# Transformer layer of a graph network: both biases of the node product added by one product over 33 rows in place of two over one row

## The chip, the cores and the metric

The kernel runs on one core of one Trainium2 chip. The metric is the device time of one execution in microseconds (us). A measurement of this kernel is the median of several executions.

## The reference

A graph with 6250 nodes of 256 features and 106250 edges, sorted by destination. Two graph convolutions and a projection come first, then a graph attention layer, and last a transformer convolution. Only that last one bears on the change:

```python
q = x1 @ Wq + bq
k = x1 @ Wk + bk
v = x1 @ Wv + bv
logits2 = jnp.einsum('ec,ec->e', q[d2], k[s2]) * scale
alpha2 = _segment_softmax(logits2, d2, n)
out = jax.ops.segment_sum(v[s2] * alpha2[:, None], d2, num_segments=n)
out = out + x1 @ Wskip + bskip
return _prelu(out, prelu2_a)
```

## The kernel before

The kernel has a preparation (`prepare`) and four layer stages, each with its own instruction blocks for the five engines and a barrier over all engines behind it: two convolutions, the attention layer, and `transformer_layer`, which is changed. The preparation loads weights and biases with a list of transfers on SP's queue, and GpSimd clears and fills the constant tiles.

In `transformer_layer` the 106250 edges, padded, are 52 groups of 16 tiles of 128 edges. GpSimd gathers the source rows of each tile with an indirect transfer (832 of them, line 1520), 16 per group, into four buffers. A body handles three groups at different ages: the scores of group k, the softmax of group k - 1 and the aggregation of group k - 2. The tensor engine walks 16 slots in a body; in each it makes a score product (line 1851, 128x257) for a tile of group k and an aggregation product (line 1862, 128x257) for a tile of group k - 2. Other steps are hung in between at slots written out by hand:

```python
if agg and s == 4:
    node_turn(n2)
...
if agg and s == 8:
    node_multiply(n2)
if chain and s == 12:
    carry_factor()
```

The bodies 0 to 2 are written out, then a loop of 12 trips has four bodies each, and the remaining ones are written out again.

Aggregation follows linearity: the weighted sum of x1 rows of a node is divided by the sum of the weights and then multiplied with Wv, so that v is never stored per edge. `an` is the normalised sum of 128 nodes with its column of weight sums (256 + 1 columns), `own` the nodes' own rows. `node_turn` transposes both (line 1826) and the last column of `an` (line 1827) into a row. Scalar copies the first into `lt` (line 1964) and the row into `sa` (line 1965). `node_multiply` then adds six products into one PSUM tile: four over 128 rows (line 1833: `lt` with Wv and with Wskip, two halves each), one over one row, `sa` with bv (line 1834), and one over one row, ones with bskip (line 1835). Each f32 product shows in the trace as two weight loads and two matmul records. Vector (`node_halves`, lines 1624 and 1625) reads the result, applies the two halves of the PReLU and adds the residual; SP stores it. Vector also makes the dot products of the scores (line 1601), one per slot, each behind its score product, and the one-hot tiles (line 1589). Scalar weighs the one-hot tiles (line 1974), evicts their transposes (line 1958) and the finished sums (line 1970); the next body's first aggregation product waits for that eviction.

There are 53 node steps: one per group and one behind the last.

Of the kernel before, what the change touches and what calls it, by code (L numbers as in the profile page):

```python
# [20 lines left out]
ACT = mybir.ActivationFunctionType  # L21
P = 128
N = 6250
E = 106250
D = 256
# [10 lines left out]
RW = D + 1  # L36
# [3 lines left out]
NGW = NC // UW  # L40
NBW = 4
QW = 4
LN_EPS = 1e-5
BIG = 1.0e30
IOA = bass.IndirectOffsetOnAxis
# [67 lines left out]
def prepare(nc, m, a):  # L113
# [9 lines left out]
    with ExitStack() as c:  # L123
# [45 lines left out]
        @block.gpsimd  # L169
        def _(pool):  # L170
            y = Tally(pool, s_hd)
            nc.gpsimd.iota(m.iota[:], [[1, P]], base=0, channel_multiplier=0, allow_small_or_imprecise_dtypes=True)
            nc.gpsimd.iota(m.iotap[:], [[1, 1]], base=0, channel_multiplier=1, allow_small_or_imprecise_dtypes=True)
            nc.gpsimd.memset(m.ones[:], 1.0)
            nc.gpsimd.memset(m.ident[:], 0.0).then_inc(s_set, 1)
            pool.wait_ge(s_set, 1)
            nc.gpsimd.affine_select(out=m.ident[:], in_=m.ident[:], compare_op=ALU.not_equal, fill=1.0,
                                    base=0, pattern=[[-1, P]], channel_multiplier=1)
            nc.gpsimd.memset(m.eps[:], LN_EPS)
            nc.gpsimd.memset(zrow[:], 0.0).then_inc(s_set, 1)  # L180
            nc.gpsimd.memset(acc[:], 0.0).then_inc(s_set, 1)

            pool.wait_ge(s_acc, 1)
            hold(m, pool)
            for k in range(2):
                pool.wait_ge(s_half[k], 16)
                for g in range(k * HG, k * HG + HG):
                    d0, = load_wide(nc, m, pool, g, ("d0",))
                    to = acc[0:1, bass.ds(d0, P)]
                    y.chain(nc.gpsimd.tensor_tensor(to, to, part[0:1, (g % HG) * P:(g % HG) * P + P], ALU.add))  # L190

        @block.sync
        def _(sp):
            sp.dma_start(dstR[:], a["dst_cols"]).then_inc(s_ld, 16)
            with nc.allow_non_contiguous_dma(reason="first destination of each group"):
                sp.dma_start(d0w[0:1, 0:NGW], a["ends"][0:1, :, 0]).then_inc(s_ld, 16)
            sp.dma_start(m.wF[:, 0:NC], a["w_cols"]).then_inc(s_ld, 16)
            sp.dma_start(nxtI[:], a["next_cols"]).then_inc(s_ew, 16)
            sp.dma_start(endI[:], a["ends"].rearrange("k g p -> g k p")).then_inc(s_ew, 16)
            for k, n in enumerate(m.ROWS):  # L200
                sp.dma_start(m.rows[:, k, :], a[n].partition_broadcast(P)).then_inc(s_w, 16)
            sp.dma_start(m.srcI[:], a["src_cols"]).then_inc(s_w, 16)
            for t_, n in WLOADS:
                sp.dma_start(t_[:], a[n].rearrange("(k p) n -> p k n", p=P)).then_inc(s_w, 16)
            with nc.allow_non_contiguous_dma(reason="a column of biases"):
                sp.dma_start(bqc[:], a["bq"].rearrange("(k p) -> p k", p=P)).then_inc(s_w, 16)
            for t_, n in ((m.bv, "bv"), (m.bsk, "bskip")):
                sp.dma_start(t_[:], a[n].rearrange("(a n) -> a n", a=1)).then_inc(s_w, 16)

            sp.wait_ge(s_sums, 2)  # L210
            with nc.allow_non_contiguous_dma(reason="the blocks of a group's own rows and columns"):
                for gi in range(TB):
                    sp.dma_start(m.wsum.rearrange("(t g a b) -> g a t b", g=TB, a=A, b=B)[gi],
                                 sums[gi * A:gi * A + A, :, gi, :]).then_inc(s_wst, 16)
            sp.wait_ge(s_wst, 16 * TB)
            sp.dma_start(part[:], m.wsum[0:HG * P].rearrange("(a n) -> a n", a=1)).then_inc(s_half[0], 16)
            sp.wait_ge(s_set, 2)
            for t_, n in ((m.t3, AGW), (m.xa, D), (m.t2, D), (m.x1, RW), (m.t4, RW), (m.qk, RW)):
                sp.dma_start(t_[NP - P:NW, :].rearrange("(k p) n -> p k n", p=P), zrow[:, :, 0:n]).then_inc(s_st, 16)
            for t_, n in ((m.t1, D), (m.h0, RW)):  # L220
                sp.dma_start(t_[NP:NW, :], zrow[:, 0, 0:n]).then_inc(s_st, 16)
            sp.wait_ge(s_hd, HG)
            sp.dma_start(part[:], m.wsum[HG * P:NGW * P].rearrange("(a n) -> a n", a=1)).then_inc(s_half[1], 16)
            sp.wait_ge(s_hd, NGW)
            sp.dma_start(m.degd.rearrange("(a n) -> a n", a=1), acc[0:1, 0:NP]).then_inc(s_ast, 16)
            sp.wait_ge(s_ast, 16)
            sp.dma_start(degT[:], m.degd.rearrange("(t n) -> t n", n=P)).then_inc(s_dg, 16)
            for j in range(NLB):
                if j in ON_ACT:
                    sp.wait_ge(s_sca, ON_ACT.index(j) + 1)  # L230
                else:
                    sp.wait_ge(s_scd, j - (j + 1) // 2 + 1)
                sp.dma_start(rows(m.t1)[:, batch(j), :], h[:, batch(j), :]).then_inc(s_st, 16)
            sp.wait_ge(s_seg, 1)
            sp.dma_start(m.rmask.rearrange("(g e) -> g e", e=3 * (P + 1)), mks[:].rearrange("g k e -> g (k e)")).then_inc(s_st, 16)
            sp.wait_ge(s_st, 16 * (8 + NLB + 1))
# [539 lines left out]
def softmax_layer(nc, m, tag, gat):  # L776
# [11 lines left out]
    with ExitStack() as c:  # L788
# [396 lines left out]
        def _(pe):  # L1185
# [27 lines left out]
            def node_multiply(n):  # L1213
                pe.wait_ge(s_lt, n + 1)
                hold(m, pe)
                if gat:
                    for j in range(2):
                        nc.tensor.matmul(psO[:, 0:RW], lt[:, j, :], m.wqk[:, j, :], start=(j == 0), stop=False)
                    last = nc.tensor.matmul(psO[:, 0:RW], m.ones[0:1, :], m.bqk[:], start=False, stop=True)
                else:  # L1220
                    for j in range(4):
                        nc.tensor.matmul(psO[:, 0:D], lt[:, j, :], (m.wv, m.wsk)[j // 2][:, j % 2, :], start=(j == 0), stop=False)
                    nc.tensor.matmul(psO[:, 0:D], sa[:], m.bv[:], start=False, stop=False)
                    last = nc.tensor.matmul(psO[:, 0:D], m.ones[0:1, :], m.bsk[:], start=False, stop=True)
                last.then_inc(s_prod, 1)

            def rows_of(bp, u):
# [228 lines left out]
def transformer_layer(nc, m):  # L1456
# [4 lines left out]
    with ExitStack() as c:  # L1461
# [9 lines left out]
        F, W, W2, M, Lp = (sb(n, [P, UW]) for n in ("F", "W", "W2", "M", "Lp"))  # L1471
        T, z = sb("T", [P, 2, UW]), sb("z", [P, UW + 1])
        run, In, Lb, Out = sb("run", [1, P + 1]), sb("In", [1, P]), sb("Lb", [1, P + 1]), sb("Out", [1, P])
        own, xa, an, lt, sa = sb("own", [P, D]), sb("xa", [P, D]), sb("an", [P, RW]), sb("lt", [P, 4, P]), sb("sa", [1, P])
        v, o, rs = sb("v", [P, D]), sb("o", [P, D]), sb("rs", [P, 1])
        psA, psT, ps, psN, psO, psR = (psb("psA", [P, 2, 512]), psb("psT", [P, 2, 512]), psb("ps", [P, 512]),
                                       psb("psN", [P, 512]), psb("psO", [P, 512]), psb("psR", [P, 512]))
# [30 lines left out]
        @block.gpsimd  # L1508
        def _(pool):
            nc.gpsimd.memset(run[:], -BIG)  # L1510
            nc.gpsimd.memset(Lb[:], -BIG)
            nc.gpsimd.memset(stage[:], 0.0).then_inc(s_zero, 1)
            for g in range(NGW):
                b = g % NBW
                if g >= NBW:
                    pool.wait_ge(s_ok, g - NBW + 1)
                for u in range(UW):
                    if g >= NBW and u % QW == 0:
                        pool.wait_ge(s_aq, (g - NBW) * NQ + u // QW + 1)
                    pool.indirect_dma_start(G[:, b, u, :], None, m.t4, IOA(ap=m.srcI[:, g * UW + u:g * UW + u + 1],  # L1520
                                                                           axis=0)).then_inc(s_g[b][u // QW], 16)
# [64 lines left out]
        def _(dve):  # L1586
# [203 lines left out]
                if agg:  # L1790
                    aggregate_more(k - 2, nwin2, xb2, xb + nwin - 1 + xb2)

            dve.wait_ge(s_zero, 1)
            dve.sem_inc(s_agx, 1)
            nc.vector.tensor_copy(relx[:, 0], m.relW[:, 0:UW]).then_inc(s_relx, 1)
            nc.vector.tensor_copy(relx[:, 1], m.relW[:, UW:2 * UW]).then_inc(s_relx, 1)
# [10 lines left out]
        def _(pe):  # L1807
# [21 lines left out]
            def node_multiply(n):  # L1829
                pe.wait_ge(s_lt, n + 1)  # L1830
                hold(m, pe)
                for j in range(4):
                    nc.tensor.matmul(psO[:, 0:D], lt[:, j, :], (m.wv, m.wsk)[j // 2][:, j % 2, :], start=(j == 0), stop=False)  # L1833
                nc.tensor.matmul(psO[:, 0:D], sa[:], m.bv[:], start=False, stop=False)  # L1834
                nc.tensor.matmul(psO[:, 0:D], m.ones[0:1, :], m.bsk[:], start=False, stop=True).then_inc(s_prod, 1)  # L1835

            def body(k, kq, kh, b):
                logits, chain, agg, lead = parts(k)
# [114 lines left out]
        def _(act):  # L1953
# [7 lines left out]
            def node(n):  # L1961
                act.wait_ge(s_turn, n + 1)
                hold(m, act)
                nc.scalar.activation(lt[:].rearrange("p j e -> p (j e)"), psN[:], ACT.Copy)
                nc.scalar.activation(sa[:], psO[0:1, 256:256 + P], ACT.Copy).then_inc(s_lt, 1)

            def finish(n):
                act.wait_ge(s_x1, n + 1)
# [57 lines left out]
                            hold(m, act)  # L2026
                            finish(n2 + i)

            act.wait_ge(s_zero, 1)
            act.sem_inc(s_ev, 1)  # L2030
            for q in range(NQ - 1):
                evict(ohT, q, 0, s_T, s_oT)
# [5 lines left out]
def build(nc, a, out):  # L2038
    with ExitStack() as c:
        sb = lambda n, s, d=F32: c.enter_context(nc.sbuf_tensor(n, s, d))  # L2040
        m = Shared()
# [5 lines left out]
        m.steps, m.rcolW = sb("steps", [P, NT]), sb("rcolW", [P, NGW + 1])  # L2047
        m.ctw = sb("ctw", [1, NGW * TW + TW], I32)
        m.wv, m.wsk = (sb(n, [P, 2, D]) for n in ("wv", "wsk"))
        m.bv, m.bsk = sb("bvr", [1, D]), sb("bskr", [1, D])  # L2050
        m.rows = sb("rows", [P, len(m.ROWS), D])
        m.row = lambda n: m.rows[:, m.ROWS.index(n), :]
        dram = lambda n, s: nc.dram_tensor(n, s, F32, kind="Internal").ap()
# [58 lines left out]
```

## Time and profile before

| what | value |
|---|---|
| median of 3 runs | 5070.54 us (5068.86 to 5072.62) |
| profiled execution, its own time | 5070.05 us |
| span of the profiled execution | 5068.3 us |
| mean granted TensorE clock over the span | 0.817 |
| tensor engine busy over the span | 75% |
| vector, scalar, GpSimd busy | 52%, 17%, 64% |

The span is the time from the first to the last instruction of the profiled execution; the execution's own time lies 1.75 us above it. Names in the rows: PE is the tensor engine's matmul, PEld its weight load, DVE vector, ACT scalar, POOL GpSimd, SP the queue of transfers. L1834 is line 1834 of the kernel. The granted clock is a share of 2.4 GHz. A busy tensor engine is not one at its peak.

### The profile page before, as it was taken

How to read it: one execution, taken by the hardware profiler on the slowest of the kernel's cores; microseconds unless marked ns; L12 is line 12 of the kernel's file. 1: busy time of each engine (PE TensorE's matmuls, PEld its weight loads, DVE VectorE, ACT ScalarE, POOL GpSimd, SP SyncE). 2: the span in 40 equal slices, each digit the busy share in tenths (PEclk: the TensorE clock that was granted, in tenths of full speed). 3: DMA queues.
4: the chain of work that ended last, by engine and by line, in shares of the span. 5: the costliest groups of instructions: out<-in, count | busy, mean ns of one | idle time of the engine just before them, and what ended most of it. 6: DMA issues, size and time to landing. Idle time of an engine off the chain costs nothing. (4 is left out here: it accounts for less than half of the span.)

```text
span 5068.3 us, 77690 instructions
## 1 busy us (share of the span) xinstructions
PE 3792.3 (75%) x16038; PEld 2830.3 (56%) x16039; DVE 2616.1 (52%) x9965; ACT 873.7 (17%) x2343; POOL 3225.0 (64%) x3401
## 2 busy tenths in 40 slices
PE   2466666666767767767688888887869888888898
PEld 2244444443444544444566666666746666666666
DVE  8544444443333333333566666666745555555554
ACT  4100000000111111111111111111113333333333
POOL 3577777776777776662776666666437665566662
PEclk7778777777777777777788888878879999999999
DMA  5544444444444444442444444444224443344332
GB/s 158 139 129 131 130 131 129 129 133 115 135 133 132 135 132 123 124 126 63 115 125 113 107 109 104 105 106 108 79 67 129 118 112 105 104 110 109 107 107 57
DMA packets 323559, 585.83 MB, mean 116 GB/s; under 512 B 82891, under 2 KB 216070, under 8 KB 322950
## 3 DMA queue, kind: packets, MB, share of 16 engines
q0 software_dynamic: 159744, 440.25, 32.3%
q1 hardware_dynamic: 144153, 125.73, 8.1%
q10 hardware_dynamic: 19056, 12.87, 0.9%
q8 instruction: 245, 4.01, 0.4%
q14 instruction: 361, 2.96, 0.2%
HBM read 514.81 MB, written 63.78 MB: 114 GB/s over the span
## 5 line engine op out<-in xcount | busy, mean ns | idle before, releaser
L558 POOL DMA_INDIRECT g_G<-t,srcI x1664 | 1589.9, 955 | 550.2 <-issue 500.5
L729 PE MATMUL g_ps<-g_G,g_oh 128*128 128x256 f32 x3328 | 981.9, 453 | 262.9 <-DMA g_G<-t,srcI 239.4
L1520 POOL DMA_INDIRECT g_G<-t,srcI x832 | 792.1, 952 | 452.0 <-PE g_ps L1862 232.3
L859 POOL DMA_INDIRECT g_G<-t,srcI x832 | 801.5, 963 | 416.6 <-issue 242.1
L729 PEld LDWEIGHTS g_ps<-g_G,g_oh 128*128 128x128 f32 x3328 | 751.6, 231 | 501.6 <-issue 260.5
L612 DVE TENSOR_SCALAR g_oh<-iota,g_relx,g_wx 128x128 f32<-128x128 f32 x1664 | 461.0, 361 | 333.4 <-PE g_ps L729 319.9
L1851 PE MATMUL g_psA<-g_win,g_ohT 128*128 128x257 f32 x1664 | 539.2, 408 | 108.9 <-issue 74.3
L1601 DVE CUSTOM_DVE_ANT_0 g_junk<-g_G,g_psA 128x257 f32<-128x257 f32 x832 | 350.9, 422 | 507.9 <-PE g_psA L1851 392.3
L1862 PE MATMUL g_ps<-g_G,g_oh 128*128 128x257 f32 x1664 | 515.0, 393 | 44.3 <-ACT g_stage L1970 44.3
L1258 PE MATMUL g_ps<-g_Gp,g_oh 128*128 128x264 f32 x1664 | 519.1, 473 | 0.0
L1258 PEld LDWEIGHTS g_ps<-g_Gp,g_oh 128*128 128x128 f32 x1664 | 385.1, 240 | 84.8
L1862 PEld LDWEIGHTS g_ps<-g_G,g_oh 128*128 128x128 f32 x1664 | 317.5, 195 | 127.0 <-ACT g_oh L1974 58.5
L1851 PEld LDWEIGHTS g_psA<-g_win,g_ohT 128*128 128x128 f32 x1664 | 285.2, 197 | 176.8 <-issue 107.0
L1239 PE MATMUL g_psA<-g_win,g_ohT 128*128 128x4 f32 x1664 | 290.3, 310 | 2.6 <-issue 2.4
L1239 PEld LDWEIGHTS g_psA<-g_win,g_ohT 128*128 128x128 f32 x1664 | 285.2, 270 | 4.5 <-issue 3.4
L619 DVE TENSOR_TENSOR g_a<-g_stage,g_own 128x256 f32<-128x256 f32 x106 | 45.3, 427 | 451.1 <-ACT g_stage L770 451.1
L1974 ACT ACTIVATE g_oh<-g_oh,g_p 128x128 f32<-128x128 f32 x832 | 253.4, 388 | 6.5
L1958 ACT ACTIVATE g_ohT<-g_psT 128x512 f32<-128x512 f32 x208 | 124.2, 597 | 751.4 <-PE g_psT L1811 751.4
L1589 DVE TENSOR_SCALAR g_oh<-iota,g_relx 128x128 f32<-128x128 f32 x832 | 246.3, 298 | 0.0
L1163 DVE TENSOR_TENSOR g_Gp<-g_G,g_psP 128x1024 f32<-128x1024 f32 x208 | 238.8, 1201 | 0.0
L770 ACT ACTIVATE g_stage<-g_ps 128x256 f32<-128x256 f32 x104 | 39.8, 383 | 1145.2 <-PE g_ps L729 1145.2
L952 DVE TENSOR_SCALAR g_oh<-iota,g_relx 128x128 f32<-128x128 f32 x832 | 180.6, 302 | 73.7 <-DVE g_run L1134 36.4
(289 smaller groups left out, 4250.0 us busy)
## 6 DMA issues: line engine op xcount, KB each, us to landing
g_G<-t,srcI POOLq DMA_INDIRECT x3328, 2.8
g_own<-t SPq DMA_DIRECT2D x159, 128.0 KB
t<-g_t SPq DMA_DIRECT2D x53, 132.0 KB
g_rec<-t SPq DMA_DIRECT2D x53, 132.0 KB
g_rec<-h SPq DMA_DIRECT2D x53, 128.5 KB
x<-g_o SPq DMA_DIRECT2D x53, 128.5 KB
g_rec<-x SPq DMA_DIRECT2D x53, 128.5 KB
t<-g_t4r SPq DMA_DIRECT2D x53, 128.5 KB
```

What stands on the lines that cost most here:

```text
L558: pool.indirect_dma_start(G[:, b, u, :], None, table, IOA(ap=m.srcI[:, g * UW + u:g * UW + u + 1], axis=0)).then_inc(s_g[b][u // QW], 16)
L612: nc.vector.tensor_scalar(oh[:, u, :], m.iota[:], relx[:, u:u + 1], wx[:, u:u + 1], ALU.is_equal, ALU.mult).then_inc(s_oh, 1)
L729: last = nc.tensor.matmul(ps[:, 0:D], oh[:, u, :], G[:, b, u, :], start=(u == 0), stop=(u == UW - 1))
L859: pool.indirect_dma_start(G[:, b, u, :], None, table, IOA(ap=m.srcI[:, g * UW + u:g * UW + u + 1], axis=0)).then_inc(s_g[b], 16)
L1239: last = nc.tensor.matmul(psA[:, u * H:u * H + H], ohT[:, u * P:u * P + P], win[:, b % 2, :], start=True, stop=True)
L1258: last = nc.tensor.matmul(ps[:, 0:RW_], lhs, rows_of(bp, u), start=(u == 0), stop=(u == UW - 1))
L1520: pool.indirect_dma_start(G[:, b, u, :], None, m.t4, IOA(ap=m.srcI[:, g * UW + u:g * UW + u + 1], axis=0)).then_inc(s_g[b][u // QW], 16)
L1589: return nc.vector.tensor_scalar(oh[:, b % 4, u, :], m.iota[:], relx[:, b % 2, u:u + 1], None, ALU.is_equal)
L1601: nc.vector.tensor_tensor_reduce(out=junk[:, u % 2, :], in0=G[:, b, u, :], in1=psA[:, u % 2, 0:RW], scale=1.0, scalar=0.0, op0=ALU.mult, o ...
L1851: nc.tensor.matmul(psA[:, u % 2, 0:RW], ohT[:, u, :], win[:, r, :], start=True, stop=True).then_inc(s_pa, 1)
L1862: last = nc.tensor.matmul(ps[:, 0:RW], oh[:, b2, u, :], G[:, b2, u, :], start=(u == 0), stop=(u == UW - 1))
L1974: last = nc.scalar.activation(src[:, u, :], src[:, u, :], ACT.Copy, scale=p[:, r, u:u + 1])
```

## The change

In the transformer layer `sa` becomes a tile of 33 rows: row 0 is the row of weight sums, row 32 holds ones, the rows between hold zeros. The two bias rows `bvr` and `bskr` become one tile `bvs` of 33 rows with bv in row 0 and bskip in row 32, zeros between. One product over the 33 rows takes the place of the two products over one row. GpSimd clears `bvs` in the preparation, and clears `sa` and sets its row 32 at the start of the layer. Vector and scalar wait for three counts of `s_zero` in place of one; SP waits for one count of `s_set` ahead of the two bias loads. (The branch with the same products in the function of the attention layer is not used by this kernel's call.)

```diff
+RB = 32
...
+            nc.gpsimd.memset(m.bvs[:], 0.0)
             nc.gpsimd.memset(m.ident[:], 0.0).then_inc(s_set, 1)
...
-            for t_, n in ((m.bv, "bv"), (m.bsk, "bskip")):
-                sp.dma_start(t_[:], a[n].rearrange("(a n) -> a n", a=1)).then_inc(s_w, 16)
+            sp.wait_ge(s_set, 1)
+            for r, n in ((0, "bv"), (RB, "bskip")):
+                sp.dma_start(m.bvs[r:r + 1, :], a[n].rearrange("(a n) -> a n", a=1)).then_inc(s_w, 16)
...
-        own, xa, an, lt, sa = sb("own", [P, D]), sb("xa", [P, D]), sb("an", [P, RW]), sb("lt", [P, 4, P]), sb("sa", [1, P])
+        own, xa, an, lt, sa = sb("own", [P, D]), sb("xa", [P, D]), sb("an", [P, RW]), sb("lt", [P, 4, P]), sb("sa", [RB + 1, P])
...
             nc.gpsimd.memset(Lb[:], -BIG)
+            nc.gpsimd.memset(sa[:], 0.0).then_inc(s_zero, 1)
+            pool.wait_ge(s_zero, 1)
+            nc.gpsimd.memset(sa[RB:RB + 1, :], 1.0).then_inc(s_zero, 1)
+            pool.wait_ge(s_zero, 2)
             nc.gpsimd.memset(stage[:], 0.0).then_inc(s_zero, 1)
...
-            dve.wait_ge(s_zero, 1)
+            dve.wait_ge(s_zero, 3)
...
-                nc.tensor.matmul(psO[:, 0:D], sa[:], m.bv[:], start=False, stop=False)
-                nc.tensor.matmul(psO[:, 0:D], m.ones[0:1, :], m.bsk[:], start=False, stop=True).then_inc(s_prod, 1)
+                nc.tensor.matmul(psO[:, 0:D], sa[:], m.bvs[:], start=False, stop=True).then_inc(s_prod, 1)
...
-                nc.scalar.activation(sa[:], psO[0:1, 256:256 + P], ACT.Copy).then_inc(s_lt, 1)
+                nc.scalar.activation(sa[0:1, :], psO[0:1, 256:256 + P], ACT.Copy).then_inc(s_lt, 1)
...
-            act.wait_ge(s_zero, 1)
+            act.wait_ge(s_zero, 3)
...
-        m.bv, m.bsk = sb("bvr", [1, D]), sb("bskr", [1, D])
+        m.bvs = sb("bvs", [RB + 1, D])
```

## Rows read from the trace of the kernel before

**Rows 1.** Page, chain that ended last, shares of the span by engine.
```profile
PE 20%; issue 3%; ACT 1%; POOL 1%; DVEq 0%; DVE 0%; ACTq 0%; DMA 0%; POOLq 0%
```

**Rows 2.** Windows, transformer layer: stretch, length, busy by engine, clock, DMA share, GB/s.
```profile
3740.00:5068.00 1328.00, 1161.89 (x5477) 887.03 (x5477) 717.47 (x3543) 431.84 (x1250) 792.66 (x835) 0.96 0.39 106
```

**Rows 3.** Chain that ended last, one node step: start, us, what, records.
```profile
4345.34 1.73 PE g_psO L1833 x8
4347.06 0.62 PE g_psO L1834 x2
4347.69 0.43 PE g_psO L1835 x2
4348.12 0.63 PE g_psA L1851 x2
4348.75 0.43 PE g_ps L1862 x2
```

**Rows 4.** The same chain, bskip product, first and last of 53.
```profile
3799.64 0.43 PE g_psO L1835 x2
...
5062.58 0.45 PE g_psO L1835 x2
```

**Rows 5.** Instructions writing psO: ns least/median/most, first and last start, form.
```profile
L1833 PE MATMUL g_psO<-wv,g_lt x212: 379/379/765, 3797.1 to 5059.2; 128*128 128x256 f32 x106
...
L1835 PE MATMUL g_psO<-bskr,ones x106: 374/374/375, 3799.5 to 5062.6; 1*128 1x256 f32 x106
```

**Rows 6.** Timeline, weight loads of that node step; in brackets idle before, releaser.
```profile
4346.99 0.29 PEld L1834 LDWEIGHTS g_psO<-bvr,g_sa 1*128 1x128 f32 x2 [0.33 <-issue]
4347.32 0.40 PEld L1835 LDWEIGHTS g_psO<-bskr,ones 1*128 1x128 f32 x2
4348.05 0.30 PEld L1851 LDWEIGHTS g_psA<-g_win,g_ohT 128*128 128x128 f32 x2 [0.33 <-issue]
```

**Rows 7.** Timeline, attention layer: the four-row load behind a one-row load.
```profile
3063.14 0.14 PEld L1347 LDWEIGHTS g_psR<-ident,g_In 4*128 4x128 f32 x1
```

**Rows 8.** Timeline, waits of vector, scalar and tensor engine within bodies.
```profile
4348.79 0.42 DVE L1601 CUSTOM_DVE_ANT_0 g_junk<-g_G,g_psA 128x257 f32<-128x257 f32 x1 [3.12 <-PE g_psA L1851]
...
4253.15 0.60 ACT L1958 ACTIVATE g_ohT<-g_psT 128x512 f32<-128x512 f32 x1 [1.14 <-PE g_psT L1811]
...
4256.49 0.67 PE L1862 MATMUL g_ps<-g_G,g_oh 128*128 128x257 f32 x2 [0.87 <-ACT g_stage L1970]
```

**Rows 9.** Chain: least and most of the mid-trip pauses, one return's, next node step.
```profile
3877.90 1.83 issue
...
4303.96 6.08 issue
...
4368.03 1.73 PE g_psO L1833 x8
...
4981.00 2.94 issue
```

**Rows 10.** Timeline, start of the transformer layer.
```profile
3740.55 0.30 POOL L1512 MEMSET g_stage<- 128x257 f32 x1
...
3741.03 0.95 POOL L1520 DMA_INDIRECT g_G<-t,srcI  x1 [0.18 <-issue]
...
3742.29 0.95 POOL L1520 DMA_INDIRECT g_G<-t,srcI  x1 [0.30 <-issue]
...
3747.77 0.42 DVE L1601 CUSTOM_DVE_ANT_0 g_junk<-g_G,g_psA 128x257 f32<-128x257 f32 x1 [3.06 <-DMA g_G<-t,srcI]
```

**Rows 11.** Timeline, start of the program: GpSimd, vector, SP's queue.
```profile
1.26 0.20 POOL L175 MEMSET ident<- 128x128 f32 x1
1.63 0.29 POOL L177 TENSOR_SCALAR_AFFINE_SELECT ident<-ident 128x128 f32<-128x128 f32 x1 [0.17 <-POOL ident L175]
...
14.60 0.69 DVE L264 TENSOR_TENSOR in_hi<-iota,in_hiF 128x512 f32<-128x512 f32 x1
...
28.03 0.33 SPq L208 DMA_DIRECT2D bvr<-bv_in  x1
```

More of the change, by code:

```diff
@@ L1222, in node_multiply @@
                         nc.tensor.matmul(psO[:, 0:D], lt[:, j, :], (m.wv, m.wsk)[j // 2][:, j % 2, :], start=(j == 0), stop=False)
-                    nc.tensor.matmul(psO[:, 0:D], sa[:], m.bv[:], start=False, stop=False)
-                    last = nc.tensor.matmul(psO[:, 0:D], m.ones[0:1, :], m.bsk[:], start=False, stop=True)
+                    last = nc.tensor.matmul(psO[:, 0:D], sa[:], m.bvs[0:1, :], start=False, stop=True)
                 last.then_inc(s_prod, 1)
@@ L1833, in node_multiply @@
                     nc.tensor.matmul(psO[:, 0:D], lt[:, j, :], (m.wv, m.wsk)[j // 2][:, j % 2, :], start=(j == 0), stop=False)
-                nc.tensor.matmul(psO[:, 0:D], sa[:], m.bv[:], start=False, stop=False)
-                nc.tensor.matmul(psO[:, 0:D], m.ones[0:1, :], m.bsk[:], start=False, stop=True).then_inc(s_prod, 1)
+                nc.tensor.matmul(psO[:, 0:D], sa[:], m.bvs[:], start=False, stop=True).then_inc(s_prod, 1)
             def body(k, kq, kh, b):
```

## The prediction

> **What bounds the kernel now.** I read the page's chain of work that ended last first: 20% of the span is the tensor engine's, 3% pauses named issue and 1% each scalar's and GpSimd's [rows 1], and the pieces are products of the transformer layer, like those of rows 3. The chain reaches back only to the start of that layer, where a barrier lies; what comes before ends at that barrier whatever this layer does. So I took a table by stage: the transformer layer runs from 3740 to 5068 us, 1328 us, and the tensor engine is busy for 1161.9 of them at a granted clock of 0.96, where vector has 717.5, scalar 431.8 and GpSimd 792.7 [rows 2]. The tensor engine, then, sets the pace of the stage that is changed. Next I read the chain through one node step. It steps from matmul to matmul with no idle piece: eight passes of the four weight products 1.73 us, the product with bv 0.62, the product with bskip 0.43, then the next edge product 0.63 and one more 0.43 [rows 3]. Those two bias products are what the change touches. The chain holds the bskip product in all 53 node steps, the first at 3799.64 us and the last at 5062.58; 52 of them stand at 0.43 us and the last at 0.45 [rows 4].
>
> **What is removed.** One product per node step, 53 in all (106 records, two passes each, median 374 ns) [rows 5]. A record's length is not its price, because passes overlap: the price is what it adds to the chain, 0.43 us, the same as any other pair of passes at this width (128x257 after 128x257 takes 0.43) [rows 3]. On the chain they are 52 x 0.43 + 0.45 = 22.81 us. They ran all at the same clock: least, median and most are 374, 374 and 375 ns [rows 5], in a stage whose granted clock is 0.96 of 2.4 GHz [rows 2].
>
> **What stays.** The 33-row product remains in the place of the bv product. Its two passes have the same 256 columns. Between one row (374 ns) and the 128-row form of the same width (median 379 ns for line 1833's [rows 5]) a 33-row pass can't be far from either: at most 5 ns by two passes by 53 = 0.5 us. I take the lower. The bv product costs 0.62 rather than 0.43 because the weight load ahead of it isn't hidden: the load engine sits idle 0.33 us before it, and again 0.33 us before the first 128-row load behind the two bias products, whose edge product costs 0.63 in place of 0.43; between the two one-row products there is no such gap [rows 3, 6]. So the going in costs 0.19 and the coming out 0.20, once each per node step, however many few-row products lie between. A four-row load behind a one-row load has no gap either [rows 7]. I take it that the 33-row product pays both: it is still not a 128-row product. No row here has 33 rows between 128-row products, so this is the open cost. Its lower bound is that both gaps vanish, 0.39 us less per step; as its upper bound I take both gaps doubled, 0.39 us more.
>
> What is late next? The shift of 0.43 us at slot 8 of a body must pass to the end of the body. Vector had waited 3.12 us for the edge product behind the bias products before its next dot, so its dot, the row maxima, the differences and with them scalar's exponential follow the tensor engine; scalar's last eviction in the body waits 1.14 us for the tensor engine's transposes; and the wait that ends the body, 0.87 us of the tensor engine for scalar's eviction of the sums, hangs on the scalar work behind that [rows 8]. All of it moves up together; none of it is anchored elsewhere. The gathers on GpSimd are issued two bodies ahead of their use and wait on the tensor engine's own progress: 1.25 us from one to the next, 20 us for a group's 16 [rows 10], under a body of 22.69 us (4368.03 less 4345.34, the node steps of two bodies [rows 3, 9]). With 0.43 us off a body they still fit. The chain's pauses named "issue" are the other candidate: some 6 us at each of the loop's 11 returns (6.2 on average over the chain), and one of 1.8 to 2.9 us (2.5 on average) in each of its 12 trips, where the vector queue stands still [rows 9]. I take both as starting when their engine gets there, so that they move with it; the rival below prices the contrary.
>
> **What is added.** (a) At the layer's start GpSimd clears sa, waits, sets row 32, waits, and only then clears stage. Today the stage memset ends and the first gather starts at 3741.03, and the chain starts with the gathers one after another, so whatever GpSimd does first is on the path in full [rows 10]. The nearest row: the identity's memset (128x128, 0.20 us) with a wait behind it, whose next instruction starts 0.37 us after it [rows 11]. Two such are 0.74 us; 0.4 (two of 0.20 with no wait behind them) and 1.1 (half as much again) bound it. Vector and scalar wait for three counts of s_zero now, which comes as late; vector's 16 one-hots and its first dot have 3.06 us of waiting for the first gather as cover, and that gather is later by the same amount [rows 10]. Behind the waiting GpSimd stand only the 832 gathers, all of them later by the 0.74. (b) In the preparation one more memset (33x256, an estimate of 0.3 us from the 0.20 of one of half the columns) delays the identity and the count that vector needs at 14.60 us, where GpSimd had it before 1.63, its wait for that count being over then [rows 11]: nothing. (c) SP waits for that same count ahead of the two bias loads, which it issues at 28.03 us [rows 11]: it finds the count there; the loads are as many and as large as before. (d) Scalar's copy into row 0 of sa is the same copy. The tables are smaller by 1 KB a partition, no work.
>
> **The sum.** Profiled execution 5070.05 us (span 5068.3 and 1.75 around it); - 22.81 + 0.74 = 5047.98. The median of the runs is 0.49 above the profiled one: 5048.5 us.
>
> **Rivals.** *Both gaps go.* If the 33-row product is run like a 128-row one, 0.39 x 53 = 20.7 us more are saved: 5027.8. For it: 33 rows are past a 32-row strip. Against: the mode seems to follow the number of rows. 0.06.
> *The gain is swallowed.* If the 1.8 to 2.9 us pause inside each loop trip ended at a time that doesn't move, it would take the 4 x 0.43 = 1.73 us that the trip gains, since it is longer than that [rows 9]: 12 x 1.73 = 20.8 us come back, 5069.3, no change that can be told. For it: the pause is there in every trip. Against: it begins when vector reaches it, just behind a skipped branch, and then the engines run on at the same spacing. 0.05.
> *The switch is dearer.* Both gaps doubled: 20.7 us come back, 5069.2; half of that, 5059. Nothing speaks for it but that the size isn't shown. 0.04.
> *Slower.* The tensor engine's own queue pauses at the loop's returns alone, some 6.2 us [rows 9]; its stream gets shorter by four instructions a body, so a skipped branch in mid-body can come to lie where its target must be fetched first, as vector's does. At the 6.2 us of the tensor engine's own pauses that is 12 x 6.2 = 74 us, 5123; at vector's 2.5, 30 us, 5079. It is slower by more than 0.2% from a pause of 2.7 us on ((10.1 + 22.1) / 12). For it: such a pause exists on vector. Against: the tensor engine shows none in twelve trips, and a branch in another place may as well lose one. 0.03.
>
> **How the numbers follow.** The forecast itself has 0.82. Its own range is 5042 to 5056: the runs before spread over 3.8 us, the loop-return pauses between 5.2 and 7.2 us, and a part of the shift may be lost in a body that waits elsewhere (13 bodies x 0.43 = 5.6 us). To the other cases the range is opened to 5040 and 5058. A measurement of this kernel can tell about 0.2%, 10.1 us, from no change. Faster (under 5060.4): 0.82, the first rival's 0.06 and half of the dearer switch, 0.90. Within: the swallowed gain and the other half, 0.07. Slower: 0.03.
>
> **What would show it.** In the changed profile the chain has 53 products of 33x256, 0.62 us each, and an edge product of 0.63 behind it; the load idles 0.33 us before both. If the chain shows 0.43 for both, the first rival is right. The first gather starts some 0.7 us after 3741.03, less what the earlier stages vary. Two node steps in mid-trip follow each other at 22.26 us in place of 22.69. The pauses keep their length of about 6.2 and 2.5 us; if the short one grew by what was saved, the gain was swallowed. A pause of the tensor engine in mid-body, or a bound of vector (no more wait before the dot behind the bias product), would make the prediction wrong.

## The result and the profile after

The changed kernel takes 5081.9 us (median of 15 runs, 5073.77 to 5087.84) beside 5072.62 us for the kernel before (median of 15, 5063.77 to 5080.94) on the same chip. The ratio is 1.0019, 95% interval 1.0011 to 1.0027: slower by 0.2%, about what a measurement of this kernel can tell, and not the 0.4% faster that was forecast. The measured time lies outside the forecast's range.

First the piece that was changed. This is the chain that ended last in the changed kernel, through one node step; line 1839 is the four weight products, 1840 the 33-row product, 1856 the score product, 1867 the aggregation product.

```profile
4354.34 1.73 PE g_psO L1839 x8
4356.07 0.63 PE g_psO L1840 x2
4356.69 0.63 PE g_psA L1856 x2
4357.32 0.43 PE g_ps L1867 x2
```

The weight loads of the same step, with the load engine's idle time before them in brackets, and the 33-row product's records over the whole layer (least, median and most ns):

```profile
4356.00 0.29 PEld L1840 LDWEIGHTS g_psO<-bvs,g_sa 33*128 33x128 f32 x2 [0.33 <-issue]
4356.62 0.30 PEld L1856 LDWEIGHTS g_psA<-g_win,g_ohT 128*128 128x128 f32 x2 [0.33 <-issue]
...
L1840 PE MATMUL g_psO<-bvs,g_sa x106: 376/480/792, 3807.0 to 5074.2; 33*128 33x256 f32 x106
```

One piece of 0.43 us is gone from the chain of [rows 3]; what remains costs what was expected: the 33-row product 0.63 us where the one-row product took 0.62, the score product behind it 0.63, and both gaps of 0.33 us of [rows 6] are there. The passes' 376/480/792 ns stand beside 374/474/791 for the one-row product of line 1834 before, so the least pass costs 2 ns more. Nothing about the 33 rows went wrong.

Next the start of the layer, on GpSimd, where [rows 10] stood before:

```profile
3747.51 0.20 POOL L1512 MEMSET g_run<- 1x129 f32 x1 [108.08 <-POOLq L87]
3747.66 0.20 POOL L1513 MEMSET g_Lb<- 1x129 f32 x1
3747.80 0.20 POOL L1514 MEMSET g_sa<- 33x128 f32 x1
3748.05 0.20 POOL L1516 MEMSET g_sa<- 1x128 f32 x1
3748.31 0.32 POOL L1518 MEMSET g_stage<- 128x257 f32 x1
3748.78 0.95 POOL L1526 DMA_INDIRECT g_G<-t,srcI  x1
```

From the first memset to the first gather it takes 1.27 us; before it was 0.77 (first memset at 3740.26, gather at 3741.03). So the two memsets with their waits cost 0.50 us, not 0.74. The whole layer begins 7.25 us later than in the profile before; two profiles of the kernel before differ there by 8.55 us (experiments, last set), so this difference can't be told from scatter.

From its first memset to the end of the span the layer takes 1332.5 us (5080.0 less 3747.51), before 1328.0 (5068.3 less 3740.26): 4.5 us more, where 22.3 less were due. (The medians differ by 9.3 us. The other 4.8 us aren't located: the two profiles can't tell them from the scatter ahead of the layer.) The windows view of the layer (stretch, length, busy time of PE, PEld, DVE, ACT, POOL, clock, DMA share, GB/s) beside [rows 2]:

```profile
3740.00:5080.00 1340.00, 1142.62 (x5377) 869.86 (x5375) 719.39 (x3543) 432.45 (x1251) 795.33 (x837) 0.94 0.39 105
```

The tensor engine is busy for 19 us less than before, as it should be, in a stretch that is longer: it waits more. The waits of the tensor engine in the layer, in us, times, and the longest, say on what:

```profile
PE g_psA L1856 <- issue: 113.0, 29, 9.8
PE g_ps L1867 <- ACT g_stage L1975: 37.7, 36, 1.4
PE g_psA L1856 <- DVE g_L L1607: 28.2, 19, 2.2
```

Those named issue, for which the profile shows no semaphore, are 113.0 us where the same view gave 74.3, all of them ahead of a score product. Against these 38.7 us more stand 12.3 us less of waits for scalar (44.3 before) and for vector (33.9 before). The chain shows where the larger part is: at the loop's returns, where [rows 9] has 6.08 us.

```profile
3908.00 9.12 issue
...
4209.92 9.07 issue
...
4413.53 6.27 issue
...
4918.55 8.70 issue
```

I sorted the time from the start of one node step's weight products to the next by the place of the body in a loop trip, and summed the tensor engine's idle time in each. Twelve trips have 48 bodies; the first trip has no return ahead of it, so 11 bodies hold one.

| body | before, mean us | changed, mean us | difference |
|---|---|---|---|
| with the loop's return (11) | 29.46 | 31.27 | +1.81 |
| first of the first trip (1) | 22.86 | 22.44 | -0.42 |
| no pause (12) | 22.85 | 22.43 | -0.43 |
| no pause (12) | 22.69 | 22.26 | -0.43 |
| with the pause of vector's queue (12) | 25.27 | 25.03 | -0.23 |
| idle of the tensor engine in a body with a return | 6.18 | 8.24 | +2.07 |

The product's 0.43 us is gained in full in every body without a pause. At each of the 11 returns the tensor engine is idle for 2.07 us more, 22.7 us in all: by chance almost the amount that 53 products save. In a return's body all but the idle time is shorter by 0.26 us and not by 0.43, 1.9 us for 11 of them: in these bodies the engine is busy for 48.7 us while the granted clock is at its lower level of 1.2 GHz, and for 45.0 before, and 3.7 us at half the clock do 1.9 us less work. Together: -22.8 for the products, +0.5 for the memsets, +22.7 at the returns, +2.7 of idle time elsewhere and +1.9 for the clock make +5.0, beside the 4.5 us measured.

### The profile page after: what moved, and what is told of

Same layout as the page of the kernel before. It is cut to its first block and busy times, and to the rows that moved or that the text cites. A ratio compares the mean times of both kernels' runs of the same rounds, so it can differ in the third digit from the quotient of the medians.

```text
span 5080.0 us, 77481 instructions
## 1 busy us (share of the span) xinstructions
PE 3791.5 (75%) x15932; PEld 2823.8 (56%) x15933; DVE 2619.3 (52%) x9965; ACT 874.6 (17%) x2343; POOL 3236.7 (64%) x3404
## 5 line engine op out<-in xcount | busy, mean ns | idle before, releaser
L732 PE MATMUL g_ps<-g_G,g_oh 128*128 128x256 f32 x3328 | 995.0, 458 | 256.4 <-DMA g_G<-t,srcI 228.8
L1856 PE MATMUL g_psA<-g_win,g_ohT 128*128 128x257 f32 x1664 | 540.3, 409 | 141.6 <-issue 113.0
```

The costliest lines, as they stand in the source:

```text
L732: last = nc.tensor.matmul(ps[:, 0:D], oh[:, u, :], G[:, b, u, :], start=(u == 0), stop=(u == UW - 1))
L1856: nc.tensor.matmul(psA[:, u % 2, 0:RW], ohT[:, u, :], win[:, r, :], start=True, stop=True).then_inc(s_pa, 1)
```

## The experiments

Theory A: the pauses named issue are the tensor engine waiting for its own program, and how long depends on where its code lies. The changed program is shorter: the compiled kernel has 9999 instructions for the tensor engine against 10067, four (two weight loads, two matmuls) fewer at each of 17 places. Two of these places lie ahead of the loop and eight in it, so the loop's end lies 40 instructions earlier. Theory B: the pause ends at a time that doesn't move with the trip, so that whatever a trip gains is waited for. Theory C: the 33-row tile, its memsets or the third wait are to blame.

**First set, four kernels.** The edit of the first, in `node_multiply` of the changed kernel:

```diff
                 nc.tensor.matmul(psO[:, 0:D], sa[:], m.bvs[:], start=False, stop=True).then_inc(s_prod, 1)
+                for _ in range(4):
+                    hold(m, pe)
```

> The changed kernel with four semaphore increments on the tensor engine's queue behind each 33-row product, one for each of the four instructions that the removed product had (two loads, two matmuls), so that the tensor engine's program is again 10067 instructions long and every later instruction lies where it lay before. The queue runs ahead of the array, so they should cost next to nothing. Theory A (the pauses at the loop's returns and in mid-trip depend on where the tensor engine's code lies): the return pause goes back from 8.2 to about 6.2 us, the two-node-step distance stays at 22.43, and the kernel is some 22 us faster than before (ratio about 0.9957). Theory B (something that doesn't move ends the pause, so that whatever a trip gains is waited for): the return pause stays at about 8 us, the ratio stays at 1.000 to 1.002.

The second is the kernel before with a shorter product:

```diff
-                nc.tensor.matmul(psO[:, 0:D], m.ones[0:1, :], m.bsk[:], start=False, stop=True).then_inc(s_prod, 1)
+                nc.tensor.matmul(psO[:, 0:1], m.ones[0:1, :], m.bsk[:, 0:1], start=False, stop=True).then_inc(s_prod, 1)
```

> The kernel before, whose bskip product is made over one column in place of 256 (the other 255 columns of bskip are left out). All instructions stay, so nothing moves in the program; the product is shorter by some 0.3 us or more of its 0.43. Theory A: pauses as before (6.2 and 2.5 us), 53 x 0.3 or more, 16 to 21 us, are gained, ratio 0.996 to 0.997. Theory B: the return pause grows by the 1.2 to 1.7 us that four bodies gain, ratio 0.999 to 1.001.

The third is the changed kernel with the increments ahead of the layer's first work only:

```diff
+            for _ in range(8):
+                hold(m, pe)
             for q in range(NQ - 1):
                 turn_hot(0, 0, q)
```

> The changed kernel with eight semaphore increments ahead of the transformer layer's first transposes on the tensor engine: the head of the loop lies where it lay before (eight instructions were removed ahead of it), the end of the loop still 32 instructions earlier. Theory A, head alone: the return pause goes back to about 6.2 us, ratio about 0.996. Theory A, but the code at the end of the trip or the blocks behind the head matter: the pause stays near 8 us or is another. Theory B: about 8 us, as the changed kernel.

The fourth is the kernel before with one product:

```diff
-                nc.tensor.matmul(psO[:, 0:D], sa[:], m.bv[:], start=False, stop=False)
-                nc.tensor.matmul(psO[:, 0:D], m.ones[0:1, :], m.bsk[:], start=False, stop=True).then_inc(s_prod, 1)
+                nc.tensor.matmul(psO[:, 0:D], sa[:], m.bv[:], start=False, stop=True).then_inc(s_prod, 1)
```

> The kernel before without the bskip product (bskip is left out): the one-row bv product alone, no 33-row tile, no memsets, no third wait. The tensor engine's program is as short as the changed one's, 9999 instructions. Theory A: as the changed kernel without the 1 us of its start, return pauses about 8.2 us, ratio 1.000 to 1.002. Theory C (the 33 rows, the memsets, the waits or SP's wait are to blame): pauses of 6.2 us, 23 us faster than before, ratio about 0.9955.

These four ran on a chip on which the kernel before takes 6225 us, so only ratios and waits can be compared. Full pad 0.997 (0.9956 to 0.9984), one column 0.9987 (0.9974 to 1.0), eight increments at the head 1.0 (0.9985 to 1.0015), bv alone 1.0004 (0.9993 to 1.0014). Bv alone has neither 33 rows nor memsets nor waits, and gains nothing for a product less: theory C falls. The padded kernel gains, and the changed kernel with eight increments at the head doesn't.

**Second set**, three of these again and a larger pad at the head (the last diff with 40 for 8), on another chip of that slow kind (6227 us):

> The padded kernel of the first set again, on whatever chip it meets; the first set met one on which the kernel before takes 6225 us and transfers are slow, and was 0.997 of it there. On a chip where the kernel before takes some 5070 us. Theory A (place of the tensor engine's code): return pause about 6.2 us and ratio about 0.9957. Theory B (a fixed end of the pause): pause about 8 us, ratio 1.000 to 1.002.

> The kernel before with the bskip product over one column (the other 255 columns of bskip left out), again. Theory A: pauses as before, ratio 0.996 to 0.997. Theory B: pauses longer by what the trip gains, ratio 0.999 to 1.001.

> The changed kernel with 40 semaphore increments ahead of the transformer layer's first transposes on the tensor engine: the end of the loop and all behind it lie where they lay before, the head of the loop 32 instructions later than before. Theory A, the head alone: the return pause differs from the 6.2 us of the kernel before and from 8.2. Theory A, the jumps near the end of the trip: the return pause is 6.2 us, ratio 0.996. Theory B: about 8 us.

> The kernel before without the bskip product (bskip left out), again: one one-row product, the tensor engine's program as short as the changed one's. Theory A and B: pauses of about 8 us as in the changed kernel, ratio 1.000 to 1.002. Theory C (33 rows, memsets, waits): pauses of 6.2 us, ratio 0.9955.

Full pad 0.9947 (0.993 to 0.9964), one column 0.9973 (0.996 to 0.9986), 40 increments 0.998 (0.9966 to 0.9994), bv alone 0.9992 (0.9981 to 1.0002). The same order as before. One column was expected at 0.996 to 0.997 and gained less, twice. On the chain its product still takes 0.12 us, so it saves 0.31 us of the 0.43, 16.4 us of 6227 or a ratio of 0.9974. Forty increments at the head were expected at 0.996 and gained less too: 19 us more than the full pad on the same chip, though the pause at the return is as short (table below).

**Third set**, with the changed kernel itself beside the padded one, and the counter-test: the kernel before, no product touched, its code moved to where the changed kernel's loop end lies.

> The changed kernel itself, so that it stands beside the others on the same chip. Ratio to the kernel before 1.000 to 1.003 by theory A and B alike. In its transformer layer the tensor engine's waits named issue should sum to some 20 to 40 us more than those of the kernel with the full pad.

> The changed kernel with four semaphore increments behind each 33-row product, third chip. Theory A (place of the tensor engine's code): 0.994 to 0.997 of the kernel before and 20 us or more faster than the changed kernel of this set; on a chip where the kernel before takes some 5070 us, return pauses of 6.2 us. Theory B: as the changed kernel.

> The kernel before, nothing changed in its products, with 216 semaphore increments ahead of the transformer layer's first transposes on the tensor engine. 216 + 40 is 256 instructions of 64 bytes, 16 KB, the mean size of a transfer of instruction queue q8 (4.01 MB in 245): the end of the loop then lies, within such a block, where it lies in the changed kernel. Theory A: the return pause grows from 6.2 to about 8 us and the kernel is 15 to 30 us slower than before (ratio 1.003 to 1.006), of which a few us may be the increments themselves at the layer's start, where GpSimd's gathers set the pace. Theory B, or a place that counts in another size of block: pauses of 6.2 us, ratio 1.000 to 1.001.

> The changed kernel with 64 semaphore increments ahead of the layer's first transposes: the loop's end comes to lie 24 instructions later than in the kernel before, farther from the place of the changed one. Theory A: as with the full pad or with 40 increments, return pause 6 to 6.5 us, ratio 0.995 to 0.998. Theory B: ratio 1.000 to 1.003.

Kernel before 6164 us: changed kernel 1.0024 (1.0006 to 1.0042), the first result over again; full pad 0.9967 (0.9948 to 0.9986), 38 us under the changed kernel on one chip; the kernel before with 216 increments 1.0092 (1.0065 to 1.0119); the changed kernel with 64 increments 1.0002 (0.9986 to 1.0019), where 0.995 to 0.998 was expected, and 21 us more than the full pad. The tensor engine's waits named issue are 56 us more in the changed kernel than in the padded one (20 to 40 expected). Of the 54 us of the 216 increments (ratio 1.003 to 1.006 expected) a good part is their own: the layer's first node step comes 140 us after its first memset, where it comes 118 us after it in the changed kernel, so 22 us; this ratio alone would prove nothing. Its return pauses do (8.27 us, table below).

**Fourth set**, on a chip of the first kind (5075 us):

> The kernel before itself, for a trace on the same chip as the next one. Theory A and B: ratio 1.000; on a chip where it takes some 5070 us, return pauses of 6.2 us on average and the transformer layer's first memset at some 3740 to 3748 us: the spread of that start tells whether the 7 us that the changed kernel's profile had lost ahead of the layer are more than the scatter from run to run.

> The changed kernel with four semaphore increments behind each 33-row product, beside a trace of the kernel before on the same chip. Theory A: return pauses within half a microsecond of those of the kernel before, every body without a pause 0.4 us shorter, ratio 0.995 to 0.997. Theory B: pauses 1.7 us longer than those of the kernel before, ratio 1.000.

The kernel before against itself 1.0 (0.9985 to 1.0015). The padded kernel 5048.65 us, ratio 0.9937 (0.9911 to 0.9962), few runs (4 of the kernel, 13 of before); 0.995 to 0.997 was expected. Its layer takes 1302.2 us from the first memset, 25.4 less than the 1327.6 of the kernel before beside it. Its tensor engine's waits, in the view that gave 113.0 for the changed kernel:

```profile
PE g_psA L1858 <- issue: 66.1, 13, 6.9
PE g_ps L1869 <- ACT g_stage L1977: 50.9, 39, 1.4
PE g_psA L1858 <- DVE g_L L1607: 35.8, 23, 2.2
```

and for the kernel before beside it:

```profile
PE g_psA L1851 <- issue: 79.2, 29, 7.2
PE g_ps L1862 <- ACT g_stage L1970: 41.7, 40, 1.4
```

The first memset of the layer lies at 3748.81 us in this profile of the kernel before, at 3746.92 in the padded one, at 3740.26 and 3747.51 in the first two: one and the same kernel, before, differs by 8.55 us here, more than the 7.25 in question.

All profiles together, by where the loop's end lies (in instructions, against the kernel before; 216 is 256 less 40): the tensor engine's idle time in a body with a return, and the pause alone, the longest idle stretch in that body; each the mean of the 11. On the slow kind of chip the body has other waits beside the pause, so that the last column is the one to compare. The kernel before wasn't profiled on a chip of the slow kind.

| kernel | loop's end | idle in the body, us | pause alone, us |
|---|---|---|---|
| before, two profiles, first kind of chip | 0 | 6.18, 6.36 | 6.18, 6.36 |
| full pad, first kind of chip | 0 | 5.81 | 5.81 |
| full pad, three profiles, slow kind | 0 | 6.56, 6.77, 7.06 | 5.85, 6.25, 5.94 |
| one column, two profiles, slow kind | 0 | 7.08, 6.99 | 6.31, 6.31 |
| changed, 40 increments, slow kind | 0 | 6.59 | 5.97 |
| changed, 64 increments, slow kind | +24 | 7.40 | 5.86 |
| changed, 8 increments, slow kind | -32 | 7.62 | 6.93 |
| changed, first kind of chip | -40 | 8.24 | 8.24 |
| changed, slow kind | -40 | 9.36 | 8.02 |
| bv alone, two profiles, slow kind | -40 | 8.42, 8.49 | 8.01, 8.13 |
| before, 216 increments, slow kind | +216 | 8.86 | 8.27 |

Whatever the products are, an end in its old place gives a pause of 5.8 to 6.4 us, an end 40 instructions earlier 8.0 to 8.2, and the kernel before shows the long pause (8.3) when 216 increments put it there. The full pad and one column make the trips shorter and keep the short pause: theory B falls. The head's place doesn't make the long pause: 40 increments at the head leave the end where it was and the head 32 instructions later, and have a short pause; 8 keep the head in place and have a longer one. With 64 increments the pause is as short as expected (5.86) and the ratio is not. So the pause at the return isn't all that a shift of the code changes: the kernels padded at the head lose some 20 us against the full pad on the same chip with pauses as short, and only some 3 us of that is the increments' own (first node step 121 us after the first memset, 118 without). Where the rest goes wasn't found.

What happens in the pause is seen in the transfers of instruction queue q8. Rows of the DMA view (queue, transfers, MB, share of its time) for four stretches of the kernel before around the return at 4201.78 us, whose pause ends at 4208.67: 4199.8 to 4201.8, 4201.8 to 4203.8, none from 4203.8 to 4205.8, and 4205.8 to 4208.7.

```profile
q8 instruction: 1, 0.02, 8.5%
q8 instruction: 1, 0.02, 5.7%
...
q8 instruction: 1, 0.02, 3.0%
```

And for the changed kernel, return at 4209.92, pause to 4218.98: 4207.9 to 4209.9, none from 4209.9 to 4211.9, 4211.9 to 4213.9, none from 4213.9 to 4215.9, and 4215.9 to 4219.0.

```profile
q8 instruction: 1, 0.02, 3.7%
...
q8 instruction: 2, 0.03, 12.5%
...
q8 instruction: 1, 0.02, 2.2%
```

For the padded kernel, return at 4200.21, pause to 4205.80: 4198.0 to 4200.0, none from 4200.2 to 4204.2, and 4204.2 to 4206.0.

```profile
q8 instruction: 2, 0.03, 10.9%
...
q8 instruction: 1, 0.02, 4.0%
```

All three have a pair of transfers, then 4 to 5 us later one more, and the tensor engine goes on when that one is over. In the kernel before, the pair begins 0.3 us before and 0.6 us behind the end of the last product; in the padded one 0.7 and 0.2 us before it; in the changed one a single transfer comes 1.1 us before it and the pair starts 2.6 and 3.0 us into the pause. So the chain of fetches at a return takes about as long in all three, and what differs is when it begins.

Read transfer by transfer, the traces say it for every return. In the four profiles from the first kind of chip all 44 pauses end within 0.7 us of the end of the third transfer, and their length goes with the time by which the last transfer before the pair begins ahead of the pause:

| last transfer before the pair, ahead of the pause by | pause, us | returns: before (two profiles) | changed | full pad |
|---|---|---|---|---|
| 8.9 to 10.0 us | 5.2 to 6.1 | 11 | 0 | 10 |
| 2.8 to 4.1 us | 6.3 to 7.2 | 11 | 3 | 1 |
| 0.2 to 1.7 us | 8.0 to 9.8 | 0 | 8 | 0 |

In all 16 profiles with their 176 returns that transfer comes less than 2.6 us ahead 47 times, and the pause is 7.5 to 9.8 us there; in the other 129 it is 7.3 us at most. Of the 47, the ends at -40 have 31 of their 44 returns, the end at +216 all 11, the end at -32 3 of 11, the ends at 0 2 of 99 and the end at +24 none. So where a fetch falls shortly ahead of the return, the pair comes late and the pause is long. That it is the fetch of the code just ahead of the return is my reading of it; which instructions a transfer carries isn't shown.

## Why the prediction was wrong, step by step

What is removed: right. 0.43 us a node step, 22.8 us; bodies without a pause are 0.43 us shorter, and with the code in its old place the kernel gains 26 us (5074.77 to 5048.65, ratio 0.9937). That 5048.65 is within 0.2 us of the forecast is luck: the kernel before is 4 us slower in that measurement, and the padded kernel's pauses are 0.5 us shorter than its.

What stays: right, both gaps are paid, 0.63 us. The first rival (both gaps go) and the dearer switch are refuted by the same rows: 33 rows cost what one row costs.

What is late next: right for vector and scalar. Vector's wait before the dot behind the bias product went from 3.12 to 2.69 us, by the 0.43, and the bodies without a pause pass all of it on.

```profile
4357.36 0.42 DVE L1607 CUSTOM_DVE_ANT_0 g_junk<-g_G,g_psA 128x257 f32<-128x257 f32 x1 [2.69 <-PE g_psA L1856]
```

What is added: 0.50 us for 0.74, a term mis-sized by 0.24 us. In the preparation the new memset takes 0.30 us, as estimated, and the bias loads are issued at 28.99 us in place of 28.03; that this costs nothing isn't shown, for it would be lost in the scatter ahead of the layer.

The step that failed is the sentence on the pauses: "I take both as starting when their engine gets there, so that they move with it." They do move with it, but I took them to keep their length: the sum has nothing for a change of the pauses at the returns. The edit moved the program whose fetches fill them, and they went from 6.18 to 8.24 us, 22.7 us in all. The rival that ended slower had the right mechanism, a shorter program whose fetches fall otherwise, but looked for a new pause in mid-body and gave it 0.03; the loop's return, where [rows 9] showed the largest wait that no semaphore explains, was the place, at 2.07 us for each of 11 returns. Its 5079 us, at vector's price for such a pause, lies nearest to the 5081.9 measured; no such pause in mid-body made it. The rival of the swallowed gain had the right amount come back (20.8 us) for a wrong reason: it looked for it at the mid-trip pause, where 0.2 us a trip went, and the padded kernel has shorter trips and pauses no longer than before.

Left open: the rule by which a place is good or bad (of five points 0 and +24 are short, -40 and +216 long, -32 lies between), which of the last jumps matters, the 2.7 us of idle time outside the returns, and the some 20 us that separate the head's pads from the full pad. Pads inside the loop alone, or a loop whose skipped parts lie elsewhere, weren't tried.

The padded kernel beats both others: it is the change plus four semaphore increments a node step on the tensor engine's queue.

## What to carry to other kernels

Here the loop's code was fetched anew around each return (three transfers of 16 KB on q8), and an edit that removed instructions moved everything behind it. Where a wait at the end of a loop has no semaphore for it, compare its length before and after, body by body, before judging the edit; a mean over the kernel hides a gain in every body and a loss at every return. If the arithmetic of an edit is right and the time isn't, put the removed instructions back as empty ones, in the places where they were: when the gain appears, it was the place of the code.

## What the runs showed of the hardware that was not expected

Moving the end of the tensor engine's loop by 40 instructions makes the pause at the loop's return some 2 us longer, and an otherwise unchanged kernel shows it too: 6.2 to 8.2 us on one kind of chip, 5.8 to 6.3 against 8.0 to 8.3 on the other. The pause ends with the last of three instruction transfers, within 0.7 us in 44 of 44 returns.

Semaphore increments on an idle tensor engine's queue aren't free: its first product comes 2.2 to 2.7 us after the layer's first memset without them, 6.4 us with 40, 10.0 us with 64 and 100.2 us with 216, where the profile shows nothing else that it waits for. Since the gathers go on meanwhile, 22 us of the last are left at the first node step. Four of them behind a product, under the array's work, cost nothing that can be seen.

The chips differ: the kernel before takes 5071 to 5076 us on some and 6164 to 6227 on others, where waits for scalar and vector of 3.5 us and more stand beside the pauses. Why they differ isn't shown. The order of full pad, one column and bv alone is the same on both chips of the slow kind that had them.
